# Edge stage of a graph network: the products that copy the basis to the lanes read 32 rows each instead of 128

## The reference

```python
p1 = jnp.tanh(p @ pp_W1 + pp_b1) @ pp_W2 + pp_b2
inter = jnp.concatenate([p1[idx_i], p1[idx_j]], axis=-1)
inter = inter @ pi_W1 + pi_b1
inter = inter @ pi_W2 + pi_b2
inter = inter @ pi_W3
inter = inter.reshape(inter.shape[0], D, N_BASIS)      # 64 x 8
i1 = jnp.einsum('ecb,eb->ec', inter, basis)            # basis: 8 numbers per edge
i1 = jnp.tanh(i1 @ ii_W1 + ii_b1) @ ii_W2 + ii_b2
out = jax.ops.segment_sum(i1, idx_j, num_segments=p1.shape[0])
```

## Time and profile before

| | us |
|---|---|
| median of 3 runs | 7844.97 |
| the profiled execution | 7882.14 |
| its span | 7880.4 |
| stretch 200 to 3700, nearly all of `edges` | 3500 |
| stretch 3900 to 7880, the dense layers | 3980 |

### The profile page before, as it was taken

How to read it: one execution, slowest core, us unless ns; L and a number is a source line. 1 busy time by engine, 2 the same in 40 slices (tenths; PEclk the granted TensorE clock), 3 DMA queues, 4 the chain that set the end, 5 groups by cost and what they waited for, 6 DMA issues and landing times.

```text
span 7880.4 us, 97479 instructions
## 1 busy us (share of the span) xinstructions
PE 6052.0 (77%) x34147; PEld 3017.3 (38%) x34147; DVE 3377.0 (43%) x9846; ACT 1314.6 (17%) x2547; POOL 3857.0 (49%) x4010
## 2 busy tenths in 40 slices
PE   4576777767777677777588888888888889898888
PEld 2233333333333333333244444444444444444444
DVE  7566666666666666666422222233222122234111
ACT  4322223223332232333200000000000000000000
POOL 3244444444444444443266466466466465564564
PEclk9688888888888888888799989899888899898899
DMA  5222223232222222222577677677677678676676
GB/s 167 80 87 90 83 87 89 86 90 83 87 88 87 89 83 87 88 88 84 168 255 245 227 245 248 231 245 241 229 252 241 226 239 268 227 251 233 222 245 197
DMA packets 793158, 1311.95 MB, mean 166 GB/s; under 512 B 235631, under 2 KB 264080, under 8 KB 792160
## 3 DMA queue, kind: packets, MB, share of 16 engines
q1 hardware_dynamic: 574188, 1096.91, 40.6%
q0 software_dynamic: 128032, 186.02, 9.3%
q10 hardware_dynamic: 90452, 22.74, 1.3%
HBM read 1136.21 MB, written 169.12 MB: 166 GB/s over the span
## 4 chain that ended last, share of the span: by engine, by line
PE 41%; issue 7%; another core or an unknown queue 3%; DVE 1%; ACT 0%; DMA 0%; DVEq 0%; ACTq 0%; SPq 0%
PE ps_a L1750 36%; PE ps_w L1778 2%; PE ps_t L1808 1%; PE ps_t L1810 1%; PE ps_t L1812 0%; PE ps_t L1822 0%; PE ps_a L1757 0%; DVE xc L1576 0%; DVE sq L1577 0%; DVE hb L1588 0%; ACT agg L1507 0%; DMA ring<-counts 0%; DVE stat L1574 0%; DVE low L1596 0%
## 5 line engine op out<-in xcount | busy, mean ns | idle before, releaser
L1750 PE MATMUL ps_a<-ring,table 128*128 128x448 fp8e4 x15092 | 3181.4, 366 | 448.5 <-issue 376.0
L1472 POOL DMA_INDIRECT got_rows<-layer_rows,tail_plan x2373 | 2266.0, 955 | 1722.5 <-issue 650.5
L731 POOL DMA_INDIRECT gathered<-u_source,plan x1568 | 1502.8, 958 | 2050.5 <-PE ps_u L944 1498.2
L1750 PEld LDWEIGHTS ps_a<-ring,table 128*128 128x128 f16 x15092 | 1491.9, 101 | 1968.7 <-issue 738.3
L855 DVE TENSOR_TENSOR z<-ps_b,u 128x1024 f32<-128x1024 f32 x784 | 932.0, 1218 | 947.8 <-PE ps_b L955 796.8
L930 PE MATMUL ps_c<-cell_hot,lane_hot 128*128 128x246 f16 x2002 | 436.5, 298 | 951.0 <-ACT unit L758 774.8
L1711 DVE TENSOR_TENSOR tail<-tail,ps_w 128x128 f32 x301 | 86.7, 288 | 2372.3 <-PE ps_w L1778 1230.0
L965 PE MATMUL ps_m<-z,M_sb 128*64 128x512 f32 x3136 | 1057.5, 785 | 0.0
L758 ACT CAST unit<-ps_c 128x490 uint16<-128x490 f32 x924 | 531.3, 575 | 1758.8 <-remote 1222.7
L930 PEld LDWEIGHTS ps_c<-cell_hot,lane_hot 128*128 128x128 f16 x2002 | 153.9, 101 | 1448.1 <-issue 1302.9
L842 DVE TENSOR_SCALAR lane_hot<-iota_n,lane,worth 128x128 f16<-128x128 f16 x2002 | 635.5, 318 | 11.8 <-issue 4.7
(11 more groups left out here) (242 smaller groups left out, 3478.3 us busy)
## 6 DMA issues: line engine op xcount, KB each, us to landing
ring<-counts SPq DMA_DIRECT2D x308, 1792.0 KB
ring<-counts SPq DMA_DIRECT2D x154, 1904.0 KB
counts<-unit SPq DMA_DIRECT2D x154, 784.0 KB
dst_all<-targets_in_ring SPq DMA_DIRECT2D x196, 256.0 KB
got_rows<-layer_rows,tail_plan POOLq DMA_INDIRECT x2373
gathered<-u_source,plan POOLq DMA_INDIRECT x1568
layer_rows<-table ACTq DMA_DIRECT2D x84, 224.0 KB
window<-u_target SPq DMA_DIRECT2D x392, 32.0 KB
```

Of the source, the lines that this page charges most:

```text
L731: pool.indirect_dma_start(gathered[q][:, i, :], None, Us, bass.IndirectOffsetOnAxis(ap=T["plan"][:, at:at + 1], axis=0)).then_inc(S[f"rows ...
L1472: pool.indirect_dma_start(got_rows[s][:, i, :], None, G["tables"][n % 2], bass.IndirectOffsetOnAxis(ap=T["tail_plan"][:, at:at + 1], axis= ...
L1750: last = mm(ps_a[:, b, 0:BC].rearrange("p (u c) -> p u c", u=BU), table[n % 2][:, k, :], cells, start=(k == 0), stop=(k == TILES - 1 and n ...
```

## The change

`which` gets 34i + h instead of 2i + h, so that `sel[:, i, :]` has its ones in rows 32i to 32i + 15 only. `load_basis` issues four transfers in place of one, each with the same 16 rows, to rows 0, 32, 64 and 96 of `basis16`. `spread` takes for product i only rows 32i to 32i + 31 of `sel` and `basis16`, which are 32 of the array's 128 rows, another quarter for each i. The wait counts 64 for four transfers. The number of products, their columns, their banks and their signals are as before.

```diff
-                    nc.vector.memset(which[:, i, h, :], float(2 * i + h))
+                    nc.vector.memset(which[:, i, h, :], float((32 + 2) * i + h))
...
                 def load_basis(g):
-                    sp.dma_start(basis16[g % 2][0:2 * NB, :], B16[:, g * EG:(g + 1) * EG]).then_inc(S[f"bas{g % 2}"], 16)
+                    for i in range(4):
+                        sp.dma_start(basis16[g % 2][32 * i:32 * i + 2 * NB, :], B16[:, g * EG:(g + 1) * EG]).then_inc(S[f"bas{g % 2}"], 16)
...
-                    pe.wait_ge(S[f"bas{q}"], 16 * (g // 2 + 1))
+                    pe.wait_ge(S[f"bas{q}"], 64 * (g // 2 + 1))
                     for p in range(2):
                         if s:
                             pe.wait_ge(S["z_done"], 2 * s + p - 1)
                         for i in range(2 * p, 2 * p + 2):
-                            last = mm(ps_b[:, i, :], T["sel"][:, i, :], basis16[q][:, HG * h:HG * h + HG], start=True, stop=True)
+                            rows = slice(32 * i, 32 * i + 32)
+                            last = mm(ps_b[:, i, :], T["sel"][rows, i, :], basis16[q][rows, HG * h:HG * h + HG], start=True, stop=True)
                         last.then_inc(S["b_done"], 1)
```

## The result

The changed kernel takes 7718.28 us, the median of 4 runs (7694.73 to 7749.56); the kernel before took 7840.67 us, the median of 4 (7834.14 to 7847.87). The ratio is 0.9846, 95% interval 0.9805 to 0.9888: 1.5% faster, 122 us. The forecast was 7801 in a range of 7715 to 7872, so the direction is right and the gain nearly three times as large as predicted; the time lies only 3 us inside the range. The profiled execution took 7749.56 us. Of all executions of this document one, of e1 at 22187.7 us, was slow; its ratio leaves it out.

The account below looks back on a forecast made before the run. It took the gathers, by holding TensorE's signals to other engines, to set the edge stage's cycle, with no engine full. The sum was 7844.97 - 44 (sixth counts) - 2.8 (last groups) + 2.8 (first loads) = 7801 us, range 7715 to 7872.

Parts of the forecast that it names:

- The bound: Edge stage: TensorE's signals come late while gathers run, held to 11.6 to 11.8 us after a group's first gather.
- The copies: Four copies side by side on TensorE save at most 0.65 us, less 0.18 us for mode changes: 0.47 us.
- Where the saving goes: Edge groups: saving stays in the gathers' shadow, except where a long group's sixth count gets through, worth about 2.2 us.
- one long group in five: Of the 98 long groups, one in five has its sixth count newly get through: 20 x 2.2 = 44 us.
- a lead in time of about 1 us: Long groups: the sixth count is issued two times 0.47 us earlier, against a wait of 7.0 us.
- The loads: SyncE's queue: three more issues a group, 0.97 us, covered by its waiting: 0 us; without cover 190 us.
- SyncE's wait for the copies: Sign on SyncE's queue: its wait should fall from 8.1 to about 7 us a group.
- The sign to look for: Casts on ScalarE: "remote" idle below 1155.6 us would say that sixth counts get through.
- longer gathers as a danger of the four loads: Prediction would be wrong if the added loads, in the gathers' first 3 us, lengthen the gathers; no size given.
- Same: Rival: the last gather alone ends the wait, whenever the count was issued; 7843 us, chance 0.28.
- Slower: Rival: four mode changes a group cost TensorE time and quarters don't overlap; 71 us, 7916; chance 0.20, drained modes 0.13.
- Much faster: Rival: 80 of 98 long groups change over, 176 us, 7669; with copies' saving on the path 7485; chance 0.10.

Follow-up runs that it names:

- e1: Changed kernel with its four basis loads and new selection pattern, but each copy again reading all 128 rows: 7888.52 us, ratio 1.001 to the kernel before.
- e8: Kernel before with every other gather left out, four a group instead of eight, the missing rows zero: 6584.74 us, ratio 0.835.
- e2: Kernel before with one load, all four copies reading rows 0 to 31 in the same quarter of the array: 7850.37 us, ratio 0.9965.
- e6: Changed kernel with the sixth count moved behind the second half of `add_up`: 7899.49 us, ratio 1.0033 to the kernel before.
- e7: Changed kernel unaltered, measured again on another chip: 7859.8 us, ratio 0.9971 to the kernel before.
- e10: Changed kernel unaltered, measured for the third time: 7725.96 us, ratio 0.9868 to the kernel before.
- e3: Changed kernel at half dose, two loads and two quarters, copies 0 and 2 sharing one, 1 and 3 the other: 7788.86 us, ratio 0.9946 to the kernel before.
- e4: Kernel before with only the sixth count moved ahead of both halves of `add_up`, copies unchanged: 7692.08 us, ratio 0.975.
- e12: Changed kernel with the sixth count ahead of both halves of `add_up`, on the same chip as e11: 7591.64 us, ratio 0.9693 to the kernel before.
- e11: e4 unaltered on another chip: 7570.88 us, ratio 0.9655 to the kernel before.

## Why the prediction was right, and where it was wrong

**The bound.** That the gathers set the cycle, by TensorE's late signals, was read from the earlier trace rows as a coincidence. e8 shows it as a cause: with four gathers instead of eight the "remote" idle goes, the held cast moves from 11.58 to 5.93 us and the cycle falls from 17.6 us to 11. What in the gathers holds the signals (their issue, what they move, or something else that eight have and four haven't) isn't shown.

**The copies.** The prediction had 0.65 us less for the four copies, less 0.18 us for going into the new mode and out of it: 0.47 us. The four themselves went from 1.03 to 0.40 us, 0.63 less, and start within 0.01 us of each other, so the quarters overlap wholly. The price is there as well: a copy behind a count starts 0.30 us after it (1999.94, 2000.24) instead of 0.21, and the first product of `add_up` starts 0.31 us after the last copy instead of 0.22 (medians). Together, 0.44 us are saved (1.07 to 0.63), close to the 0.47. This term was right in all its parts, and e2 shows the price by itself, 0.19 us. The Trainium skill (TensorE: Matmul & The Clock Gate, "Measured speedup vs the span model") says that four row tiles of 32 rows and 512 columns ran 3.07 times as fast as one after the other. The trace agrees in kind: from the first copy's start to that of the next product it was 0.86 us (2011.71, 2012.57) and is 0.33 us (2000.24, 2000.57), 2.6 times as fast.

**Where the saving goes.** Two steps of the argument held. The saving is not on the path by itself (e6: none of it left), and it pays through sixth counts that get through, at about 2.2 us each on the mean (measured 18.54 - 16.43 = 2.1 within one trace, 2.47 against the held groups of before). The term that was mis-sized is "one long group in five, 20 x 2.2 = 44 us". 36 of 93 more were early, two in five, worth 0.96 x 98 = 94 us; with 20 us for the held ones and 12 us of loss in the short ones that is 103. The forecast's own range for this number, 5 to 45, holds it; the time that went with that range, 7746 to 7834, doesn't hold 7718, and the wider range does by 3 us. "One in five" was a guess, and with the very same kernel e7 gave 25 us and e10 101: that the first measurement fell inside the range was in part luck.

**What makes a count early.** I argued with a lead in time of about 1 us, two times 0.47. The measured lead is half of that: the sixth count ends 4.73 us after the first gather instead of 5.26 (medians of the long groups). The saving of the four copies beside the first gather is mostly gone before the next four: in the short groups the third count behind the first gather ends at 2.94 us instead of 3.09. That the lead helps, the dose says: with the count's place unchanged, ends at 5.26 (before), 4.93 (e3) and 4.69 us (e10) go with 4, 11 and 39 early groups. That it isn't the whole, e4 and e6 say: at the same 5.3 us 63 get through where the count stands ahead of `add_up`, and at 5.0 us none where it stands behind it. Within the change itself the earliest don't fare best: of 16 sixth counts that end before 4.45 us 2 get through, of 64 between 4.45 and 5.0 us 38, of 13 later ones none. So the step "an earlier count gets through" was too simple, and why e7 had only 22 stays open with it.

**The loads.** 0 us predicted, and none to be told from nothing in e1. SyncE's wait for the copies should fall from 8.1 to about 7 us a group; it is 1293.5 / 188 = 6.9. All loads and this wait (400 to 3600 us), against the earlier trace rows:

```profile
L685 SPq DMA_DIRECT2D basis<-basis_halves x784: 302/420/1986, 301.2 to 3612.5; - x196
```

```profile
SPq L685 <- PE ps_b L957: 1293.5, 188, 9.9
```

**The sign to look for.** "Remote" idle before the casts below 1155.6 us was a bad sign to name: it is 1164.4 in a kernel 1.5% faster. In an early group the sixth count's cast is no longer held to the end, but it still waited 5.52 us, and there are 885 casts in the stretch instead of 858. The right sign is the time of the sixth count's cast in each long group, and how many of them come before 11.0 us.

**What was not foreseen.** Copies side by side have a price that the prediction hasn't got: e6 lost 21 to 26 us, up to 9 of them for another reason, and e12 is 21 us behind e11. One thing that goes with it is longer gathers. With eight gathers in a group, the kernels with four quarters have a mean of 970 to 977 ns, all others of 955 to 965. It isn't every gather that grows. Sorted by their place in the group (groups 4 to 189), the last of the eight takes 1118 ns instead of 1016, and 60 of 186 take more than 1.3 us instead of 18; the first seven grow by 4 ns on the mean. The prediction named longer gathers as a danger of the four loads; e1 has the loads, 957 ns and again 18 such last gathers, so they alone don't do it. A group's last gather so ends 0.13 us later on the mean, about the 0.12 us by which the short groups grew, but that is not yet a cause: the cast that waits for the gathers' end in the short groups comes only 0.04 us later (11.74 instead of 11.70), and the rest of the growth lies behind it; between e11 and e12 it is 0.04 and 0.15 us. The clock is lower too, e12 has 0.83 where e11 has 0.86. What makes the loss stays open.

**The rivals.** "Same" is excluded in the first measurement and in e10, and nearly true on the chip of e7. "Slower" by drained modes is excluded: the price of the modes is there (0.19 us for four copies in e2), but the quarters overlap, and the two together still save 0.44 us. "Much faster" needed 80 of 98 groups; only the moved count came there.

## What to carry to other kernels

When a faster instruction lies in the shadow of something else, look for the one signal that just misses getting out and ask what it would take to issue it earlier. Here moving one line (the sixth count ahead of `add_up`) gave 2.5 to 3.5%, and making the work in front of it 2.6 times as fast gave 0.3 to 1.5%. A gain that hangs on a near miss can differ from chip to chip and from run to run. Count in the trace how often the event happens and look at how its times are spread, since a single threshold hides it, measure on more than one chip, and distrust a change whose own runs scatter twice as far as those of the kernel before.

## What the runs showed of the hardware

- While GpSimd issues eight indirect gathers, TensorE's signals to other engines come late, at the latest some 11.5 to 11.8 us after the first gather in the kernel before. The last gather's record ends at 9.7 us. The Trainium skill (Perfetto Trace Analysis, "DMA Instruction — SWDGE (GPSIMD)") says that such a record ends when the last descriptor is written and not when the data has moved; the 1.9 us between the two agree with that. The trace shows it directly: the last landing of a gather recorded in a group comes at 12.0 us (median of the groups of the kernel before). With four gathers (record of the last ends at 4.7 us) the held cast comes at 5.9 us, and the "remote" idle of the casts is 11.9 us of 2100 instead of 1155.6 of 3200.
- Whether such a signal gets out depends on its place in TensorE's order and not on its time alone: of counts that end 5.0 us or more after the first gather, 0 of 62 got through between the halves of `add_up` and 42 of 67 ahead of them (before, e4).
- Four copies of 32 rows in four quarters of the array take 0.40 us, in two quarters 0.60, in one 1.03, as with all 128 rows.
- Changing from products of 128 rows to products of 32 and back costs 0.19 us (e2: 1.16 against 0.97 us across four copies that are no shorter).
- Reading 32 rows instead of 128, in copies that are no shorter, goes with a granted clock of 0.80 instead of 0.83 between 200 and 3600 us (e2 against before and e1). Over the whole kernel it is 0.852 to 0.856 in all 8 executions of e2 and 0.863 to 0.870 in the 20 of the kernel before beside them.
- When the four quarters are used, the last of eight indirect gathers takes longer, 1118 ns against 1016 on the mean, and not when the four loads alone are there (1011).
